# A two-layer graph network on one core: edges counted in 32 groups of 32 targets instead of 16 groups of 64

## What is computed

```python
h = (x @ W1).reshape(n, 8, 768)                  # 768 -> 6144 columns
alpha_s, alpha_d = sum(h * a_src), sum(h * a_dst)
e = leaky_relu(alpha_s[src] + alpha_d[dst], 0.2)
e = exp(e - segment_max(e, dst)[dst]); alpha = e / segment_sum(e, dst)[dst]
h = elu(segment_sum(h[src] * alpha, dst) + b1)   # then a second attention layer with W2
x = layernorm(x + attention(x)); x = layernorm(x + gcn(x))
```

## Time and profile before

| | us |
|---|---|
| median of 3 runs | 1667.49 (1666.68 to 1670.44) |
| the profiled execution | 1668.99 |
| its span, first to last instruction | 1667.2 |
| PE busy | 1640.6 (98%) |
| DVE busy | 1239.5 (74%) |
| ACT busy | 769.6 (46%) |
| POOL busy | 156.5 (9%) |

### The profile page before, as it was taken

How to read it: one execution, slowest core, us unless ns; L and a number is a source line. 1 busy time by engine, 2 the same in 40 slices (tenths; PEclk the granted TensorE clock), 3 DMA queues, 4 the chain that set the end, 5 groups by cost and what they waited for, 6 DMA issues and landing times. The chain is left out here.

```text
span 1667.2 us, 21294 instructions
## 1 busy us (share of the span) xinstructions
PE 1640.6 (98%) x7491; PEld 1368.3 (82%) x7504; DVE 1239.5 (74%) x2378; ACT 769.6 (46%) x1215; POOL 156.5 (9%) x126
## 2 busy tenths in 40 slices
PE   7999999999999999999999999999999999999998
PEld 6777788888878888888888888888888887979898
DVE  7777656754998888788778788877886668785447
ACT  3222222322465565556556556655655535644340
POOL 1212123222200000000000000000000001031003
PEclk9999999999999999999999999999999999999999
DMA  7444455894656576467547466754844547023122
GB/s 256 152 152 152 152 179 194 190 259 161 204 171 179 185 199 155 158 190 193 124 177 218 165 167 189 188 124 172 217 139 158 189 161 186 24 89 105 57 93 98
DMA packets 135327, 271.82 MB, mean 163 GB/s; under 512 B 24234, under 2 KB 83508, under 8 KB 122676
## 3 DMA queue, kind: packets, MB, share of 16 engines
q1 hardware_dynamic: 133968, 267.26, 53.1%
q0 software_dynamic: 1152, 3.15, 1.0%
q10 hardware_dynamic: 100, 0.03, 0.0%
HBM read 210.01 MB, written 60.40 MB: 162 GB/s over the span
## 5 line engine op out<-in xcount | busy, mean ns | idle before, releaser
L41 PE MATMUL psum<-ph,hc 128*128 128x512 f32 x768 | 299.4, 390 | 2.2 <-DVE pl L1039 1.2
L43 PE MATMUL psum<-ph,hc 128*128 128x512 f32 x768 | 298.8, 389 | 0.0
L42 PE MATMUL psum<-pl,hc 128*128 128x512 f32 x768 | 298.8, 389 | 0.0
L41 PE MATMUL psum<-wh,xTh 128*128 128x512 f32 x570 | 225.0, 395 | 0.0
L978 DVE CUSTOM_DVE_ANT_0 junk<-psum,a_bc 128x512 bf16<-128x512 f32 (+1 forms) x256 | 129.9, 554 | 127.4 <-ACT st L618 119.1
L43 PE MATMUL psum<-wh,xTl 128*128 128x512 f32 x570 | 222.2, 390 | 0.0
L42 PE MATMUL psum<-wl,xTh 128*128 128x512 f32 x570 | 221.9, 389 | 0.0
L618 ACT CAST st<-psum 128x512 fp32r<-128x512 f32 x96 | 56.6, 589 | 286.7 <-PE psum L43 280.5
L41 PEld LDWEIGHTS psum<-ph,hc 128*128 128x128 f32 x768 | 144.1, 188 | 33.9 <-DVE pl L1039 2.1
L43 PEld LDWEIGHTS psum<-ph,hc 128*128 128x128 f32 x768 | 144.1, 188 | 30.0
L42 PEld LDWEIGHTS psum<-pl,hc 128*128 128x128 f32 x768 | 144.2, 188 | 29.7
(11 more groups left out here) (285 smaller groups left out, 3116.2 us busy)
## 6 DMA issues: line engine op xcount, KB each, us to landing
hc<-h_scratch SPq DMA_DIRECT2D x96, 1024.0 KB, 6.1
h_scratch<-st SPq DMA_DIRECT2D x96, 512.0 KB, 3.2
w2r<-in_L_gnn_W SPq DMA_DIRECT2D x96, 384.0 KB, 6.8
wr<-in_L_gnn_W SPq DMA_DIRECT2D x12, 1536.0 KB, 8.4
gwr<-in_L_gnn_W SPq DMA_DIRECT2D x24, 384.0 KB, 3.4
row_bc<-logits_scratch SPq DMA_DIRECT2D x16, 512.0 KB, 13.5
expo_bc<-expo_scratch SPq DMA_DIRECT2D x16, 512.0 KB, 6.2
xr<-in_x SPq DMA_DIRECT2D x2, 1536.0 KB, 10.4
```

Source lines behind the costliest of these rows:

```text
L41: nc.tensor.matmul(out, sh, mh, start=first, stop=False, skip_group_check=not grouped)
L42: nc.tensor.matmul(out, sh, ml, start=False, stop=False, skip_group_check=not grouped)
L43: return nc.tensor.matmul(out, sl, mh, start=False, stop=last, skip_group_check=not grouped)
```

## The change

The groups are half as wide and there are twice as many: `WD` = 32, so 32 groups; four firm tiles (`FIRM` = 4) and the loop's two make six slots. `hot_key` of a tile has 8 x 32 = 256 columns, so the count matmuls are 128x256; `hot_low`'s firm instruction makes 4 tiles, not 8; ACT copies 128x256. Group w is made by DVE behind block w + 1, whole and in one piece, and counted by PE behind block w + 3, so that each of the blocks 3 to 34 has a group behind it. PE now reads a group's number of pairs right behind the group before it. For the reference's edges each group of 32 needs 3 pairs of tiles, except group 10 (541 edges that start in tile 39 and end in tile 44), which needs 4: 194 count matmuls.

There are still 16 pairs of semaphores; groups w and w + 16 share one. POOL clears the first eight pairs at the head of its chunk 2 and the other eight at the head of chunk 3, and counts each clearing on a new semaphore, `hot_cleared`. DVE waits for it before groups 16 and 24, PE before it signals for these groups, behind groups 14 and 22.

```diff
-WD = 64
+WD = 32
 NW = N // WD
-TG = 8
-FIRM = 8
+FIRM = 4
 SLOTS = FIRM + 2
+HOT_SEMS = 16
...
-    HOT_A = {2 * w + 1: w for w in range(NW)}
-    HOT_B = {2 * w + 2: w for w in range(NW)}
-    COUNT_AFTER = {2 * w + 4: w for w in range(NW)}
+    HOT_AT = {w + 1: w for w in range(NW)}
+    COUNT_AFTER = {w + 3: w for w in range(NW)}
...
             for q in range(QN - 1):
+                if q in (2, 3):
+                    pool.wait_ge(count_out, 8 * (q - 1))
+                    for w in range(8 * (q - 2), 8 * (q - 1)):
+                        pool.sem_clear(hot_ready[w % HOT_SEMS]).then_inc(hot_cleared, 1)
+                        pool.sem_clear(hot_free[w % HOT_SEMS]).then_inc(hot_cleared, 1)
...
-            def hot_begin(w, first):
-
+            def hot(w):
+
+                first = dve.value_load(range_i[w:w + 1, 0:1], min_val=0, max_val=ET - SLOTS)
+                pairs = dve.value_load(range_i[w:w + 1, 1:2], min_val=FIRM // 2 + 1, max_val=EP)
+                if w >= HOT_SEMS and w % 8 == 0:
+                    dve.wait_ge(hot_cleared, HOT_SEMS * (w // 8 - 1))
                 if w >= 2:
                     dve.wait_ge(count_full, w - 1)
...
+                for j in range(FIRM):
+                    nc.vector.tensor_scalar(hot_key[w % 2][:, j, :], lane[:, :], keyT[:, bass.ds(first + j, 1)], float(-NB * WD * w),
+                                            ALU.subtract, ALU.is_equal).then_inc(hot_ready[w % HOT_SEMS], 1)
                 with dve.Fori(FIRM // 2, pairs) as q:
-                    dve.wait_ge(hot_free[w], q * 2 + 2)
+                    dve.wait_ge(hot_free[w % HOT_SEMS], q * 2 + 2)
...
-                    if j == 0 and 2 <= w + 1 < NW:
-                        mm.then_inc(hot_free[w + 1], SLOTS)
+                    if j == 0 and w + 2 < NW:
+                        mm.then_inc(hot_free[(w + 2) % HOT_SEMS], SLOTS)
                 with pe.Fori(FIRM // 2, pairs) as q:
                     for j in range(2):
-                        pe.wait_ge(hot_ready[w], q * 3 + (j - 1))
+                        pe.wait_ge(hot_ready[w % HOT_SEMS], q * 3 + (j + 1))
...
+                    if n in COUNT_AFTER:
+                        count(COUNT_AFTER[n], pairs)
                     if n + 1 in COUNT_AFTER:
                         w = COUNT_AFTER[n + 1]
                         pairs = pe.value_load(range_i[w:w + 1, 1:2], min_val=FIRM // 2 + 1, max_val=EP)
-                    if n in COUNT_AFTER:
-                        count(COUNT_AFTER[n], pairs)
```

More of the change, by code:

```diff
@@ L160, in graph_and_layers @@
     parts_i = put("parts_i", early + 1024, [P, 2, 2, P], I32)
-    lanes = put("lanes", 180224, [P, P, TG], I16)
+    lanes = put("lanes", 180224, [P, P, FIRM], I16)
     key16 = put("key16", 182272, [P, 2 * P], I16)
@@ L174, in graph_and_layers @@
     touch = put("touch", late + 3072, [P, 2, NW], F32)
-    win_f = put("win_f", late + 3200, [P, NW], F32)
-    lane = put("lane", late + 3264, [P, NB * WD], F16)
+    win_f = put("win_f", late + 3328, [P, NW], F32)
+    lane = put("lane", late + 3456, [P, NB * WD], F16)
     zero_b = put("zero_b", late + 4288, [P, 512], BF16)
@@ L249, in graph_and_layers @@
     low_hot, lanes_made = sem("low_hot"), sem("lanes_made")
-    hot_ready = [sem(f"hot_ready{w}") for w in range(NW)]
-    hot_free = [sem(f"hot_free{w}") for w in range(NW)]
+    hot_ready = [sem(f"hot_ready{w}") for w in range(HOT_SEMS)]
+    hot_free = [sem(f"hot_free{w}") for w in range(HOT_SEMS)]
+    hot_cleared = sem("hot_cleared")
     count_full, count_out = sem("count_full"), sem("count_out")
@@ L362, in count_bank @@
     def count_bank(w):
-        return banks[6 + w % 2]
+        return banks[6 + w % 2][:, 0:NB * WD]
     with nc.Block() as block:
@@ L941, in hot_begin @@
                 nc.vector.tensor_tensor(hot_low[w % 2][:, :, 0:FIRM], lanes[:, :, :],
[L942 to L948, removed]
+                                        key16[:, bass.ds(first, FIRM)].unsqueeze(1).to_broadcast([P, P, FIRM]), ALU.is_equal).then_inc(hot_ready[w % HOT_SEMS], 1)
+                for j in range(FIRM):
+                    nc.vector.tensor_scalar(hot_key[w % 2][:, j, :], lane[:, :], keyT[:, bass.ds(first + j, 1)], float(-NB * WD * w),
+                                            ALU.subtract, ALU.is_equal).then_inc(hot_ready[w % HOT_SEMS], 1)
                 with dve.Fori(FIRM // 2, pairs) as q:
-                    dve.wait_ge(hot_free[w], q * 2 + 2)
+                    dve.wait_ge(hot_free[w % HOT_SEMS], q * 2 + 2)
                     nc.vector.tensor_tensor(hot_low[w % 2][:, :, FIRM:SLOTS], lanes[:, :, 0:2],
-                                            key16[:, bass.ds(q * 2 + first, 2)].unsqueeze(1).to_broadcast([P, P, 2]), ALU.is_equal).then_inc(hot_ready[w], 1)
+                                            key16[:, bass.ds(q * 2 + first, 2)].unsqueeze(1).to_broadcast([P, P, 2]), ALU.is_equal).then_inc(hot_ready[w % HOT_SEMS], 1)
                     for j in range(2):
                         nc.vector.tensor_scalar(hot_key[w % 2][:, FIRM + j, :], lane[:, :], keyT[:, bass.ds(q * 2 + first + j, 1)], float(-NB * WD * w),
-                                                ALU.subtract, ALU.is_equal).then_inc(hot_ready[w], 1)
+                                                ALU.subtract, ALU.is_equal).then_inc(hot_ready[w % HOT_SEMS], 1)
             for g in range(FB):
@@ L1079, in _ @@
                             x_low(g)
[L1080 to L1085, removed]
+                    if n in HOT_AT:
+                        hot(HOT_AT[n])
                     if (q, b) in TURNED_AT:
@@ L1501, in count @@
                     pe.wait_ge(count_out, w - 1)
+                if HOT_SEMS <= w + 2 < NW and w % 8 == 6:
+                    pe.wait_ge(hot_cleared, HOT_SEMS * ((w + 2) // 8 - 1))
                 for j in range(FIRM):
-                    pe.wait_ge(hot_ready[w], j + 2)
-                    mm = nc.tensor.matmul(bank[:, :], hot_low[w % 2][:, :, j], hot_key[w % 2][:, j, :],
+                    pe.wait_ge(hot_ready[w % HOT_SEMS], j + 2)
+                    mm = nc.tensor.matmul(bank, hot_low[w % 2][:, :, j], hot_key[w % 2][:, j, :],
                                           start=(j == 0), stop=False, skip_group_check=True)
-                    if j == 0 and 2 <= w + 1 < NW:
-                        mm.then_inc(hot_free[w + 1], SLOTS)
+                    if j == 0 and w + 2 < NW:
+                        mm.then_inc(hot_free[(w + 2) % HOT_SEMS], SLOTS)
                 with pe.Fori(FIRM // 2, pairs) as q:
                     for j in range(2):
-                        pe.wait_ge(hot_ready[w], q * 3 + (j - 1))
-                        nc.tensor.matmul(bank[:, :], hot_low[w % 2][:, :, FIRM + j], hot_key[w % 2][:, FIRM + j, :],
-                                         start=False, stop=False, skip_group_check=True).then_inc(hot_free[w], 1)
+                        pe.wait_ge(hot_ready[w % HOT_SEMS], q * 3 + (j + 1))
+                        nc.tensor.matmul(bank, hot_low[w % 2][:, :, FIRM + j], hot_key[w % 2][:, FIRM + j, :],
+                                         start=False, stop=False, skip_group_check=True).then_inc(hot_free[w % HOT_SEMS], 1)
                 nc.tensor.matmul(bank[:, 0:P], zero_b[:, 0:P], zero_b[:, 0:P], start=False, stop=True, skip_group_check=True).then_inc(count_full, 1)
```

8 lines of the change are left out of this document (4 added, 4 removed).

## The result

The changed kernel takes 1656.32 us (median of four runs, 1656.20 to 1658.04) against 1667.62 us of the kernel before, measured beside it (four runs, 1666.68 to 1670.44): a ratio of 0.9931, with an interval of 0.9917 to 0.9945. It is 11.3 us faster; 9.5 were predicted. The profiled execution took 1656.4 us with a span of 1654.6.

The account below looks back on a forecast made before the run. PE bounds the kernel; its groups' 39.6 us fall to 28.2 + 0.2 + 1.0 + 0.7 = 30.1, a gain of 9.5 us that takes the median from 1667.49 to 1658.0 us, range 1654.5 to 1664.0.

Parts of the forecast that it names:

- what could be played for: All groups' cost on PE in the stage before the change: 16 x 2.38 + 1.50 = 39.6 us.
- The matmul of half the columns: PE's count matmuls: 256 columns cost 0.108 us each, on the line between 0.054 (128 columns) and 0.215 (512).
- The bound of 0.137: Upper bound for a count matmul on PE: 0.137 us if records of `hot_low` weight loads did not overlap; chance 0.09.
- The fixed part of a group: Paid once a group on PE: 0.06 us at the loop's entry plus 0.17 for closing matmul and slow return.
- Group 10: Group with one pair more on PE: 0.22 us for it, 1.0 stall on DVE, 0.7 for the open reading.
- rival E: PE's sequencer loses its lead every step, the reading stands open 0.5 us, 32 times: 16 us, 1674; chance 0.05.
- Its step: DVE's work per block and group: 3.7 us, or 4.7 with POOL's lock in three steps of four, against PE's 4.96.
- Rival C: DVE becomes the pacemaker at 5.93 us a step, deciding from about 5.1: 1683.5 us; chance 0.04.
- Costed at nothing: ACT's 32 half-width copies and POOL's clearings, done at 104.5 us before PE needs them: no cost.
- rival F: PE gives the saved time back to a later wait, or small openings in groups sum to it: 1667.5; chance 0.06.

Follow-up runs that it names:

- e2: Changed kernel, but each count matmul is cut into two of 128 columns, each with its own load of `hot_low`: 1659.04 us, ratio 0.9941.
- e1: Changed kernel, but each count matmul streams its 256 columns twice, so 512 again, with the 32 groups kept: 1679.14 us, ratio 1.0058.
- e3: Changed kernel, but PE reads the next group's number of pairs ahead of the group, not behind it: 1657.63 us, ratio 0.9930.
- e4: Changed kernel, but DVE makes each firm `hot_key` once more into a spare buffer nobody reads: 1664.99 us, ratio 0.9977.
- e9: Changed kernel, but DVE makes each firm `hot_key` twice and PE reads the next number of pairs ahead of the group: 1662.62 us, ratio 0.9965.
- e8: Kernel before with its 16 groups, but DVE makes each in one piece behind block 2w + 1: 1669.25 us, ratio 0.9999.
- e5: Changed kernel, but DVE makes each firm `hot_key` twice more into a spare buffer nobody reads: 1687.72 us, ratio 1.0113.

## Why the prediction held, and where its steps were off

**The bound, and what could be played for.** The groups were put at 39.6 us on PE before, and that is what they cost. That time saved on PE in this stage comes off the end held too: 10.95 us in the stage, 11.0 at the end of the aggregation. Of the 11.3 us between the medians the last 0.3 are within the scatter behind the stage.

**The matmul of half the columns.** 0.108 us was forecast, 0.109 measured. The bound of 0.137 from the loads' records had no substance (e2), and e1 gives the whole effect back and more. The row chosen, loads of 98 ns at a distance of 54 ns, was the right one.

**The fixed part of a group** was the term that was off. It was taken over from before as 0.06 + 0.17 = 0.23 us. Now it is 4.91 - 4.08 - 6 x 0.109 = 0.18: 0.04 for the entry instead of 0.06, the rest 0.14 instead of 0.17. Over 32 groups that is 1.5 us, the difference between 9.5 and 10.95. About 0.01 of the 0.05 is rounding: by the third decimal a matmul of 512 columns took 0.216 us before, which leaves 0.22 for the fixed part. The columns do not make the rest: e1 has 512 again, and pays 5.55 - 4.08 - 6 x 0.216 = 0.17. Nor does the place of PE's reading: e3 has it elsewhere, and steps of 4.91 as well. A part can be seen on PE: behind a group the block's first to its last matmul took 59.49 - 55.50 = 3.99 us before and takes 53.16 - 49.20 = 3.96 now. What makes it shorter stays open.

**Group 10** was put at 0.22 + 1.0 + 0.7 = 1.9 us, and is 1.94. Its parts are right as well: the reading costs 0.65 us there (e3) and nothing in 31 other places. So rival E fell. That the sequencer's lead is the reason is borne out by e4, where DVE is late and the same reading stands open thirteen times.

**DVE.** Its step was put at 3.7 us, and 4.7 with POOL's lock, against 4.96. Here it is in the changed kernel, DVE's timeline and the slice beside it:

```profile
49.29 0.69 DVE L979 CUSTOM_DVE_ANT_0 junk<-psum,a_bc 128x512 bf16<-128x512 f32 x1 [0.85 <-ACT st L623]
...
51.12 0.85 DVE L945 TENSOR_TENSOR hot_low<-lanes,key 128x512 bf16<-128x512 int16 x1
51.89 0.86 DVE L948 TENSOR_SCALAR hot_key<-lane,keyT 128x256 bf16<-128x256 f16 x4
52.68 0.32 DVE L952 TENSOR_TENSOR hot_low<-lanes,key 128x256 bf16<-128x256 int16 x1
52.88 0.47 DVE L955 TENSOR_SCALAR hot_key<-lane,keyT 128x256 bf16<-128x256 f16 x2
...
54.20 0.69 DVE L979 CUSTOM_DVE_ANT_0 junk<-psum,a_bc 128x512 bf16<-128x512 f32 x1 [0.85 <-ACT st L623]
```

```profile
50.40 1.29 POOL L574 TENSOR_TENSOR wl<-wr,wh 128x512 fp32r<-128x512 f32 x1 [3.62 <-ACT wh L591]
```

The step is 4.91 us with 0.85 of it idle, so 4.06 of work with a lock; a `hot_key` takes 0.20 us ((52.68 - 51.89)/4), as put. The lock costs about 0.4 here (`hot_low` has 0.77 us to the next instruction, 0.35 where no slice lies beside it), not 1.0, since DVE reaches `hot_low` when POOL's slice is more than half done. The Trainium skill ("SBUF — State Buffer", "Who interferes with whom") says that the lock is held for a whole instruction. The three rows agree: `hot_low` is done 0.20 us behind the end of the slice, whenever it began (51.89 against 51.69 here, 133.31 against 133.10 in e9, 134.63 against 134.43 in e4).

**Rival C was right to fall, but its point was put wrongly.** It was said to decide from about 5.1 us a step, on the average over steps with and without a slice. e4 has 3.65 + 4 x 0.196 = 4.4 us of work a step without a lock, and 5.2 on that average if three steps in four pay 1.0; a small loss was to be expected, and 7.1 us came. The average is the wrong measure. A step with a slice costs PE its whole excess (5.24 - 4.91 = 0.33 us in e9), and the next one without a slice does not run below PE's 4.91, so it gives nothing back. In e9 the thirteen steps with a slice have 4.4 us of excess between them and the one with DVE's opening 0.8, 5.2 in all, against 5.2 measured (4.6, and the 0.65 that e9 saves at group 10). In e4 the reading behind the group adds 0.13 us to each of the fourteen ((2.5 - 0.65)/14). And the price of a lock depends on the phase: 0.4 us while DVE is early, 0.9 once it is late, after group 10's stall. So an estimate from these steps is that C decides where DVE's own work passes 4.91 - 0.9 = 4.0 us; runs stand only on either side of it, at 3.65 and 4.3. The changed kernel is some 0.35 us away from that, where the prediction saw 1.4 (5.1 against 3.7). That C did not come is therefore in part luck: there was room, but a quarter of what the prediction counted on. The opening of 1.7 us that DVE's two readings make at the end of chunk 2 was not foreseen either; in rival C they were to stand open in every step, for 0.9.

**Costed at nothing.** The first eight pairs of POOL's clearings (its sequencer's record of L560, one of the two in a pair, first and last start):

```profile
L560 POOLq EVENT_SEMAPHORE_RANGE_CLEAR  x8: 44/44/48, 96.5 to 98.0; - x8
```

These sixteen clearings take from 96.5 to 98.1 us and are over long before PE comes to block 17; no wait on them shows in any view. ACT's 32 narrower copies wait for PE, and nobody for them.

**Nothing was given back later** (rival F): the stage's 10.95 us are still there at the last matmul, which comes 12.6 us sooner in the first trace of the changed kernel and 11.0 in the second. Traces of one kernel differ by up to 1.6 us there.

**The order on DVE** that the change also makes was not costed on its own; it is worth nothing (e8).

## What to carry to other kernels

When work on the bounding engine is halved in size and doubled in count, split its cost into the part that goes with size and the part paid once a piece, both from distances between starts and not from lengths of records: here 0.215 to 0.109 us a matmul, and 0.18 us a group. For an engine beside it that must keep pace, take the step that comes again and again, not the average, and with the contention at the phase it would have when late. A single longer step does no harm while the engine is ahead (5.75 us once in the changed kernel), and costs its excess once it is behind. A reading into a register is free as long as the sequencer is ahead; put it in front of the wait that takes the lead away, not behind it.

## What the runs showed of the hardware

- A weight load whose record is 125 ns long is hidden under matmuls 55 ns apart, also with columns that lie apart in memory (e2).
- DVE and POOL can lock into step. POOL's slice follows ACT's copy, which follows PE's block, so once DVE is late its `hot_low` meets the slice at the same point, in e9 in five steps and then in six of a chunk's eight, and the lateness sustains itself (steps of 5.2 us instead of 4.91).
- Two readings of `range_i` behind a wait that had stopped DVE's sequencer left DVE idle for 1.67 us (changed kernel, group 22); one reading on PE behind such a wait cost 0.65 us (e3). In the other steps the reading on PE cost nothing that the steps of 4.91 us would show.
- The granted clock of PE fell to 0.50 twice in e5, for about 3 us, after openings of 0.27, 0.28 and 0.45 us close together, or of 0.70 and 0.50. The openings of 0.70 and 0.44 us at group 10 of the changed kernel did not bring it down. Why the one and not the other, these runs don't tell.
